# First unit's chain from o to x1 taken batch by batch, weight loads with two semaphores, last expert's add on VectorE, new order tables

## The chip, the cores and the metric

The kernel runs on one core of a Trainium2 chip. The metric is the device time of one execution in microseconds; the median of three runs of the kernel before is 577.14 us. Five engines work side by side, each through its own list in order, and meet at semaphores: TensorE (PE), VectorE (DVE), ScalarE (ACT), GpSimd (POOL) and SyncE (SP), which issues the loads and stores.

## The reference

One decoder layer over x of 16 batches x 128 positions x 256 features. Three parts, each added to its input and normalised:

```python
# attention, 16 heads of 16: causal scores, the 32 largest of each row kept, softmax over them
q, k, v = x @ Wq.T + bq, x @ Wk.T + bk, x @ Wv.T + bv
scores = where(causal, -inf, einsum('bhqd,bhkd->bhqk', q, k) / 4)
attn = softmax(keep_top_32(scores))
x1 = layernorm(x + (attn @ v) @ Wo.T + bo)
# eight experts of 256 -> 512 -> 256, summed with gates of (context, token kind)
h = relu(einsum('edi,bsi->bsed', proj_in, x1)); o = einsum('eid,bsed->bsei', proj_out, h)
gate[e] = sum over k of ctx[b, s, k] where itok[b, k, s] == e
x2 = layernorm(x1 + einsum('bsei,bse->bsi', o, gate))
# Hadamard transform, 4 bit quantised activations, ternary weight
xh = x2 @ H; q = clip(round(xh / scale), -8, 7) * scale
out = layernorm(x2 + q @ ternary(weight).T)
```

## The kernel before

The 16 batches are taken two at a time, in eight **units** v = 0 to 7. A unit has four attention **tiles** k (batch, half of the heads; name 0.3 here for tile 3 of unit 0). A tile goes through scores (PE), copy_scores (ACT), first_max and seven `select` stages of top-8 steps (DVE), exp (ACT), keep (DVE), turn_probs (PE), copy_probs (ACT), attend (PE), normalise (DVE). With all four tiles done the unit has o, and a chain leads to x1: turn_o (PE transposes, recorded at L758), copy_ot (ACT, L653), out_proj (PE, L750), ln1_stats (DVE, L993), rstd1 (POOL, L559), ln1_apply (ACT, L580 and L584), turn_x1 (PE, L758), x1t_high (ACT, L662), x1t_low (DVE, L1019): the last two give x1 transposed as a sum of two float16 parts. Then sixteen expert steps L1 (with relu on ACT and h_low on POOL) alternate with sixteen L2; each is twelve matmuls of 128x256. The gate is applied by gate_out (ACT) and summed by gated_add (POOL), expert by expert. The output part (ln2_stats to store, `OUT_STEPS`) of a unit runs beside the next unit's experts; for the last unit it is done one batch at a time.

K and V of units ahead are computed early into a ring of six (`AHEAD`). The projections, attention outputs, transposes, and the output part share one PSUM bank `ps_misc`: each PE step that takes it waits until the last user has been read (`take_misc`). In the first unit the expert weights are prepared too: load_w (SP) fetches both matrices of an expert into one of two staging buffers, w_squares (ACT, L694) sums their squares, w_sum (PE, L881) adds over partitions, w_scale (DVE, L1041) makes a power of two, w_high (ACT) and w1_low, w2_low (POOL) split the weights in two float16 parts. A buffer is loaded again when both low parts of the expert in it are done.

The order is written out by number: tables `STEADY`, `FIRST` (unit 0), `SECOND`, `LAST`, `FINAL` (last batch) give each step a slot relative to the unit, `PREP` and `AHEAD` those of the weights and of K and V. `build_schedule` places all steps, sorts by slot, and each engine takes its own in that order. No table changes what is computed. The first expert step of a unit waits for `x1t_low`:

```python
if e == 0 and z == 0:
    pe.wait_ge(x1t_low, v + 1)
```

## Time and profile before

| | us |
|---|---|
| three runs, median | 577.14 |
| lowest, highest of them | 575.81, 581.07 |
| profiled execution | 578.48 |
| its span | 576.7 |
| TensorE busy | 524.5 |
| VectorE busy | 444.2 |
| ScalarE busy | 413.6 |
| GpSimd busy | 349.8 |
| mean granted clock of TensorE | 0.964 of full |

The profiled execution has 1.8 us around its span. Busy shares are averages: the program has a ramp in which the first unit's attention and the weights are prepared, a long middle with expert matmuls, and a tail with the output part of the last unit. So the page is read first for the share of each engine and the granted clock by slice, then the windows for the three stages, then the timeline for single steps.

### The profile page before, as it was taken

How to read it: one execution, taken by the hardware profiler on the slowest of the kernel's cores; microseconds unless marked ns; L12 is line 12 of the kernel's file. 1: busy time of each engine (PE TensorE's matmuls, PEld its weight loads, DVE VectorE, ACT ScalarE, POOL GpSimd, SP SyncE). 2: the span in 40 equal slices, each digit the busy share in tenths (PEclk: the TensorE clock that was granted, in tenths of full speed). 3: DMA queues.
4: the chain of work that ended last, by engine and by line, in shares of the span. 5: the costliest groups of instructions: out<-in, count | busy, mean ns of one | idle time of the engine just before them, and what ended most of it. 6: DMA issues, size and time to landing. Idle time of an engine off the chain costs nothing.

```text
span 576.7 us, 22355 instructions
## 1 busy us (share of the span) xinstructions
PE 524.5 (91%) x8180; PEld 449.3 (78%) x8180; DVE 444.2 (77%) x2842; ACT 413.6 (72%) x1004; POOL 349.8 (61%) x358
## 2 busy tenths in 40 slices
PE   4857678999999999999999999999999999999953
PEld 3545557888888888888888888888888888888841
DVE  2798979778889987998899878989899899413114
ACT  3888878766767678768867777778776778567541
POOL 2578556974647565656566654757465746486762
PEclk9878799999999999999999999999999999999985
DMA  7354432000100010000200010002001000000000
GB/s 212 133 167 128 162 116 58 21 3 1 40 19 5 3 35 8 21 3 3 76 20 4 2 59 3 3 3 75 4 3 40 1 21 3 3 1 19 2 18 18
DMA packets 21949, 21.85 MB, mean 38 GB/s; under 512 B 1872, under 2 KB 19792, under 8 KB 21840
## 3 DMA queue, kind: packets, MB, share of 16 engines
q1 hardware_dynamic: 21840, 20.42, 11.4%
q8 instruction: 65, 1.06, 0.8%
q14 instruction: 44, 0.36, 0.2%
HBM read 18.32 MB, written 2.10 MB: 35 GB/s over the span
## 4 chain that ended last, share of the span: by engine, by line
PE 75%; ACT 4%; issue 4%; POOL 3%; DVE 2%; POOLq 0%; ACTq 0%; DVEq 0%
PE ps_o L871 27%; PE ps_z L855 26%; PE ps_misc L750 6%; PE ps_pt L818 5%; PE ps_s L798 4%; PE ps_misc L828 3%; PE ps_misc L733 2%; PE ps_misc L758 2%; POOL h_lo L526 2%; ACT h_raw L674 1%; POOL acc L547 1%; ACT x L580 0%; PE ps_s L807 0%; POOL rstd L565 0%; DVE t L993 0%
## 5 line engine op out<-in xcount | busy, mean ns | idle before, releaser
L526 POOL TENSOR_TENSOR h_lo<-h_raw,h_hi 128x512 f16<-128x512 f32 x128 | 149.2, 1166 | 129.6 <-ACT h_raw L674 128.7
L871 PE MATMUL ps_o<-w_hi,h_lo 128*128 128x256 f16 x512 | 139.7, 273 | 3.4 <-POOL h_lo L526 3.4
L855 PE MATMUL ps_z<-x1t_hi,w_lo 128*128 128x256 f16 x512 | 139.9, 273 | 1.1 <-DVE x1t_lo L1019 1.1
L855 PE MATMUL ps_z<-x1t_lo,w_hi 128*128 128x256 f16 x512 | 139.6, 273 | 0.0
L871 PE MATMUL ps_o<-w_hi,h_hi 128*128 128x256 f16 x512 | 139.6, 273 | 0.0
L871 PE MATMUL ps_o<-w_lo,h_hi 128*128 128x256 f16 x512 | 139.6, 273 | 0.0
L855 PE MATMUL ps_z<-x1t_hi,w_hi 128*128 128x256 f16 x512 | 139.6, 273 | 0.0
L670 ACT ACTIVATE h_hi<-ps_z 128x512 f16<-128x512 f32 x128 | 75.6, 591 | 53.8 <-PE ps_z L855 53.8
L963 DVE MATCH_REPLACE8 taken<-next,taken 128x64 f32<-128x64 f32 (+4 forms) x480 | 110.7, 243 | 0.7 <-issue 0.7
L547 POOL TENSOR_TENSOR acc<-go_sb,acc 128x512 f32<-128x512 f32 x56 | 71.2, 1272 | 32.4 <-ACT go_sb L684 32.4
L958 DVE MAX8 next<-taken 128x8 f32<-128x64 f32 (+4 forms) x480 | 85.4, 245 | 0.0
L674 ACT ACTIVATE h_raw<-ps_z 128x512 f32<-128x512 f32 x128 | 75.6, 590 | 0.0
L637 ACT ACTIVATE pt_sb<-ps_pt 64x512 f32<-64x512 f32 x64 | 37.9, 592 | 34.6 <-PE ps_pt L818 34.2
L684 ACT ACTIVATE go_sb<-ps_o,gate 128x256 f32<-128x256 f32 x128 | 53.4, 470 | 11.3 <-PE ps_o L871 10.0
L871 PEld LDWEIGHTS ps_o<-w_hi,h_lo 128*128 128x128 f16 x512 | 50.0, 98 | 12.3 <-POOL h_lo L526 4.6
L855 PEld LDWEIGHTS ps_z<-x1t_hi,w_lo 128*128 128x128 f16 x512 | 50.1, 98 | 8.2 <-DVE x1t_lo L1019 1.6
L871 PEld LDWEIGHTS ps_o<-w_lo,h_hi 128*128 128x128 f16 x512 | 50.1, 98 | 6.7
L855 PEld LDWEIGHTS ps_z<-x1t_lo,w_hi 128*128 128x128 f16 x512 | 50.1, 98 | 5.9
L871 PEld LDWEIGHTS ps_o<-w_hi,h_hi 128*128 128x128 f16 x512 | 50.1, 98 | 5.8
L855 PEld LDWEIGHTS ps_z<-x1t_hi,w_hi 128*128 128x128 f16 x512 | 50.1, 98 | 5.8
L629 ACT ACTIVATE ps_s<-s_sb,neg_max 128x48 f32<-128x48 f32 (+2 forms) x192 | 51.5, 317 | 0.0
L932 DVE MAX8 top<-s_sb 128x8 f32<-128x16 f32 (+7 forms) x256 | 37.5, 218 | 11.7 <-ACT s_rev L614 11.7
(138 smaller groups left out, 991.2 us busy)
## 6 DMA issues: line engine op xcount, KB each, us to landing
w_raw<-in_w1t SPq DMA_DIRECT2D x8, 512.0 KB, 3.9
w_raw<-in_w2t SPq DMA_DIRECT2D x8, 512.0 KB, 5.0
xt_sb<-in_xt SPq DMA_DIRECT2D x8, 256.0 KB, 3.1
x_sb<-in_x SPq DMA_DIRECT2D x8, 256.0 KB, 3.5
xa_sb<-in_xt SPq DMA_DIRECT2D x7, 256.0 KB, 3.4
out<-out_sb SPq DMA_DIRECT2D x7, 256.0 KB, 2.5
ctx_sb<-in_ctx_w SPq DMA_DIRECT2D x8, 128.0 KB, 3.4
itok_sb<-in_itok SPq DMA_DIRECT2D x8, 128.0 KB, 2.9
```

What stands on the lines that cost most here:

```text
L526: nc.gpsimd.tensor_tensor(h_lo[:, e % 2, 2 * z:2 * z + 2, :], h_raw[:, z, :, :], h_hi[:, e % 2, 2 * z:2 * z + 2, :], ALU.subtract)\
L547: nc.gpsimd.tensor_tensor(acc[:, :, :], go_sb[:, e % 2, :, :], prev[:, :, :], ALU.add)\
L629: last = act.activation(dst, s_sb[:, k % 2, score_at(j):score_at(j) + m], ACT.Exp, bias=neg_max[:, k % 2, j:j + 1], scale=SCALE)
L637: act.activation(pt_sb[0:rows, k % 2, :, HALF * half:HALF * (half + 1), :].rearrange("p h j q -> p j h q"), ps_pt[0:rows, :].rearrange("p ...
L670: act.activation(h_hi[:, e % 2, 2 * z:2 * z + 2, :], ps_z[z][:, :].rearrange("p (c t) -> p c t", c=2), ACT.Relu)\
L674: act.activation(h_raw[:, z, :, :], ps_z[z][:, :].rearrange("p (c t) -> p c t", c=2), ACT.Relu)\
L684: last = act.activation(go_sb[:, e % 2, b, :], ps_o[e % 2][:, b * D:(b + 1) * D], ACT.Copy, scale=gate[:, b, e:e + 1])
L855: last = pe.matmul(ps_z[z][:, d * UT:(d + 1) * UT], w[:, e, c, at:at + P], x[:, c, :], start=n == 0, stop=n == len(terms) - 1)
L871: last = pe.matmul(ps_o[e % 2][:, b * D:(b + 1) * D], h[:, e % 2, c, b * SEQ:(b + 1) * SEQ], w[:, e, c, :], start=n == 0, stop=n == len(te ...
L932: last = V.max(top8[:, k % 2, j, :], s_sb[:, k % 2, score_at(j):score_at(j) + QB * (j + 1)])
L958: last = V.max(next8[:, j, :], t)
L963: last = V.match_replace(t, next8[:, j, :], t, TAKEN)
```

## The change

Five edits. (1) In unit 0 the nine steps of the chain from turn_o to x1t_low (`IN_STEPS`) are done once for batch 0 and once for batch 1, each on its half (`INS`); batch 0's stand in a table of their own, `EARLY`. The other units do them whole, as before; waits that counted units count chains (`chains`). The first expert step waits for both halves. (2) load_w has a semaphore for each of its two loads; the first is issued once w1_low is done, w_squares waits for each when it needs it. (3) In the last unit the eighth expert is scaled and added by VectorE straight from PSUM, one batch at a time (`gated_last`), instead of gate_out on ScalarE and gated_add on GpSimd. (4) For the last unit's two outputs `ffn_residual` moves from GpSimd to VectorE. (5) All tables have new numbers, and each expert's preparation has an offset of its own (`at0` to `at7`).

```diff
+INS = [(0, b, 1) for b in range(UB)] + [(v, 0, UB) for v in range(1, UNITS)]
...
+FINISH = SLOTS + 1
...
+EARLY = STEADY | {
+    "turn_o": 27, "copy_ot": 26, "out_proj": 27.75, "ln1_stats": 27, "rstd1": 33.5, "ln1_apply": 30.5,
+    "turn_x1": 32.5, "x1t_high": 31.75, "x1t_low": 33.5, "ffn": 64, "exp": 4.5, "to_q4": 63.5, "v": 121.25,
...
+    "ffn_abs": -24, "ffn_sum": 40.75, "ffn_ternary": 42.75, "at0": 1.75, "at1": 1, "at2": 0.5, "at3": -0.5,
...
-    ("sp", "load_ctx"), ("sp", "load_x"), ("pool", "x_plus_bo"), ("pe", "turn_o"), ("act", "copy_ot"),
-    ("pe", "out_proj"), ("dve", "ln1_stats"), ("pool", "rstd1"), ("act", "ln1_apply"), ("pe", "turn_x1"),
-    ("act", "x1t_high"), ("dve", "x1t_low"), ("dve", "gate_scale"),
+    ("sp", "load_ctx"), ("sp", "load_x"), ("pool", "x_plus_bo"), ("dve", "gate_scale"),
 )
+IN_STEPS = (
+    ("pe", "turn_o"), ("act", "copy_ot"), ("pe", "out_proj"), ("dve", "ln1_stats"), ("pool", "rstd1"),
+    ("act", "ln1_apply"), ("pe", "turn_x1"), ("act", "x1t_high"), ("dve", "x1t_low"),
+)
+ON_DVE = ("ln3_apply", "ffn_residual")
...
@@ -209,6 +225,10 @@
             elif z == 1:
+                if v == SPLIT and e == EXPERTS - 1:
+                    for b in range(UB):
+                        put(base + at["experts"] + FINISH + b / 8, "dve", "gated_last", v, b)
+                    continue
                 put(s + at["gate_out"], "act", "gate_out", v, e)
@@ -227,10 +247,14 @@
                 put(base + at[name], engine, name, v)
+        for i in (0, 1) if v == 0 else (v + 1,):
+            table = EARLY if i == 0 else at
+            for engine, name in IN_STEPS:
+                put(base + table[name], engine, name, i)
         for o in (v,) if v < SPLIT else (v, v + 1):
...
             for engine, name in OUT_STEPS:
-                put(base + at[name], "dve" if name == "ln3_apply" and v == SPLIT else engine, name, o)
+                put(base + at[name], "dve" if name in ON_DVE and v == SPLIT else engine, name, o)
         if v > 0:
@@ -239,7 +263,7 @@
                 first = max(0, first - PREP_SLOTS * STAGED + max(PREP["w1_low"], PREP["w2_low"]) - PREP["w_squares"])
-            put(first + PREP[name], engine, name, 0, e)
+            put(first + PREP[name] + PREP[f"at{e}"], engine, name, 0, e)
     for engine, name in (("act", "ffn_abs"), ("pe", "ffn_sum"), ("dve", "ffn_ternary")):
@@ -410,10 +436,14 @@
-            if name in OUT_NAMES:
-                _, first, count = OUTS[v]
+            if name in OUT_NAMES or name in IN_NAMES:
+                _, first, count = (OUTS if name in OUT_NAMES else INS)[v]
                 return slice(first, first + count), count
...
+
+        def chains(v):
+
+            return v + 1 if v > 0 else 0
@@ -462,9 +492,9 @@
                     wait(sp, w1_low_ready, e - STAGED + 1)
+                    sp.dma_start(w1_raw[:, e % STAGED, :, :], rows(w1t[e])).then_inc(w1_loaded[e % STAGED], 16)
                     wait(sp, w2_low_ready, e - STAGED + 1)
-                    sp.dma_start(w1_raw[:, e % STAGED, :, :], rows(w1t[e])).then_inc(w_loaded[e % STAGED], 16)
-                    sp.dma_start(w2_raw[:, e % STAGED, :, :], rows(w2t[e])).then_inc(w_loaded[e % STAGED], 16)
+                    sp.dma_start(w2_raw[:, e % STAGED, :, :], rows(w2t[e])).then_inc(w2_loaded[e % STAGED], 16)
                 elif name == "store":
@@ -639,9 +669,10 @@
                 elif name == "ln1_apply":
-                    wait(act, x1t_ready, v)
-                    wait(act, acc_done, EXPERTS * (v - 1) + 1)
-                    layernorm_apply(0, x1, t1, v, x1_ready)
+                    unit = INS[v][0]
+                    wait(act, x1t_ready, chains(unit))
+                    wait(act, acc_done, EXPERTS * (unit - 1) + 1)
+                    layernorm_apply(0, x1, t1, v, x1_ready, batches(name, v)[0])
                 elif name == "ln3_apply":
@@ -649,9 +680,10 @@
                         act.wait_ge(s_vo, 64)
+                    at = columns(batches(name, v)[0])
                     for c in range(CD):
-                        last = act.activation(ot_sb[:, c, :], ps_misc[:, c * UT:(c + 1) * UT], ACT.Identity,
-                                              bias=bv_sb[:, c:c + 1])
+                        last = act.activation(ot_sb[:, c, at], ps_misc[:, c * UT + at.start:c * UT + at.stop],
+                                              ACT.Identity, bias=bv_sb[:, c:c + 1])
                     last.then_inc(ot_copied, 1)
@@ -690,9 +722,10 @@
                     e, = args
-                    act.wait_ge(w_loaded[e % STAGED], 32 * (e // STAGED + 1))
+                    act.wait_ge(w1_loaded[e % STAGED], 16 * (e // STAGED + 1))
                     act.activation(w1_hi[:, e, :, :], w1_raw[:, e % STAGED, :, :], ACT.Square,
                                    accum_out=w_sq[:, e, 0:1])
+                    act.wait_ge(w2_loaded[e % STAGED], 16 * (e // STAGED + 1))
                     act.activation(w2_hi[:, e, :, :], w2_raw[:, e % STAGED, :, :], ACT.Square,
@@ -831,19 +864,20 @@
                 elif name == "turn_o":
-                    pe.wait_ge(o_ready, TILES * (v + 1))
-                    turn(o_sb, ident, ot_ready, ps_misc)
+                    bs, _ = batches(name, v)
+                    pe.wait_ge(o_ready, TILES * INS[v][0] + GROUPS * bs.stop)
+                    turn(o_sb, ident, ot_ready, ps_misc, bs)
                 elif name == "out_proj":
                     pe.wait_ge(ot_copied, v + 1)
-                    rows_by([ot_sb], wo_sb, y_ready)
+                    rows_by([ot_sb], wo_sb, y_ready, batches(name, v)[0])
                 elif name == "turn_x1":
                     pe.wait_ge(x1_ready, v + 1)
-                    turn(x1, ident, x1t_ready, ps_misc)
+                    turn(x1, ident, x1t_ready, ps_misc, batches(name, v)[0])
                 elif name == "L1":
...
                     if e == 0 and z == 0:
-                        pe.wait_ge(x1t_low, v + 1)
+                        pe.wait_ge(x1t_low, chains(v + 1))
                     if v == 0:
@@ -988,12 +1022,14 @@
                     dve.wait_ge(y_ready, v + 1)
-                    dve.wait_ge(xb_ready, v + 1)
-                    wait(dve, x1_ready, v)
-                    V.tensor_tensor(t1[:, :, :], ps_misc[:, :].rearrange("p (b n) -> p b n", b=UB),
-                                    xb_sb[:, :, :], ALU.add).then_inc(t1_ready, 1)
+                    unit = INS[v][0]
+                    dve.wait_ge(xb_ready, unit + 1)
+                    wait(dve, x1_ready, chains(unit))
+                    bs, _ = batches(name, v)
+                    V.tensor_tensor(t1[:, bs, :], ps_misc[:, :].rearrange("p (b n) -> p b n", b=UB)[:, bs, :],
+                                    xb_sb[:, bs, :], ALU.add).then_inc(t1_ready, 1)
                     dve.wait_ge(t1_ready, v + 1)
-                    layernorm_stats(0, t1, v)
+                    layernorm_stats(0, t1, v, bs)
                 elif name == "gate_sums":
@@ -1053,6 +1089,20 @@
                             .then_inc(w_undo_step, 1)
+                elif name == "gated_last":
+                    b, = args
+                    dve.wait_ge(l2_done, RING_STEPS * (v + 1))
+                    dve.wait_ge(acc_done, EXPERTS * v + EXPERTS - 1)
+                    V.scalar_tensor_tensor(acc[:, b, :], ps_o[(EXPERTS - 1) % 2][:, b * D:(b + 1) * D],
+                                           gate[:, b, EXPERTS - 1:EXPERTS], acc[:, b, :], ALU.mult, ALU.add)\
+                        .then_inc(last_added, 1)
+                elif name == "ffn_residual":
+                    bs, _ = batches(name, v)
+                    dve.wait_ge(f_scaled, v + 1)
+                    V.tensor_tensor(t3[:, bs, :], f_sb[:, bs, :], x2[:, bs, :], ALU.add).then_inc(t3_ready, 1)
+                elif name == "ln2_stats" and v >= SPLIT:
+                    dve.wait_ge(last_added, v - SPLIT + 1)
+                    layernorm_stats(1, acc, v, batches(name, v)[0])
                 elif name == "ln2_stats":
```

Where the order moves, at three places. VectorE in the first unit, from the weight scale before the projection's sum to x1t_low; names: `w_ms` is w_scale, `t` with `xb_sb` and `stats` are ln1_stats, `top` is first_max, `p_sb` is keep, `next`, `taken` and `dropped` are select. Before:

```order
L1047 TENSOR_SCALAR w_pow<-w_half 128x2
L993 TENSOR_TENSOR t<-ps_misc,xb_sb 128x512
L908 BN_STATS stats<-t 128x6 x2
L913 BN_AGGR meanvar<-stats 128x2 x2
L932 MAX top<-s_sb 128x8 x8
L972 SCALAR_TENSOR_TENSOR p_sb<-dropped,ps_s 128x48
L974 SCALAR_TENSOR_TENSOR p_sb<-taken,ps_s 128x576
L954 MAX next<-s_rev 128x8
...
L958 MAX next<-taken 128x8 x5
L1019 TENSOR_TENSOR x1t_lo<-ps_misc,x1t_hi 128x512
```

Of the change, the same place (batch 1's half):

```order
L1083 TENSOR_SCALAR w_pow<-w_half 128x2
L1029 TENSOR_TENSOR t<-ps_misc,xb_sb 128x256
L942 BN_STATS stats<-t 128x6
L947 BN_AGGR meanvar<-stats 128x2
L997 MATCH_REPLACE taken<-next,taken 128x64
...
L1006 SCALAR_TENSOR_TENSOR p_sb<-dropped,ps_s 128x48
L1008 SCALAR_TENSOR_TENSOR p_sb<-taken,ps_s 128x576
L966 MAX top<-s_sb 128x8 x8
L988 MAX next<-s_rev 128x8
...
L992 MAX next<-taken 128x8 x5
L1055 TENSOR_TENSOR x1t_lo<-ps_misc,x1t_hi 128x2x128
```

The sum and statistics have half the columns and stand one select stage earlier; between them and x1t_low there is that stage, keep, a first maximum and two select stages. Batch 0's halves stand earlier in the list: the statistics behind the second gate sum, the low part behind the first maximum of the second unit and the weight scale of expert 5.

TensorE in the first unit, from attend of tile 1 to the projection of batch 0 (`wv_sb` is V, `wk_sb` K, `w_sq` a weight sum, `ps_pt` turn_probs). Before:

```order
L828 MATMUL ps_misc<-v_sb,pt_sb 32x17 x32
L733 MATMUL ps_misc<-xa_sb,wk_sb 128x256 x4
L818 MATMUL ps_pt<-ident,p_sb 128x128 x4
L750 MATMUL ps_misc<-wv_sb,xa_sb 128x256 x4
L818 MATMUL ps_pt<-ident,p_sb 128x128 x4
L881 MATMUL ps_o<-w_sq,ones 128x2
```

Of the change:

```order
L861 MATMUL ps_misc<-v_sb,pt_sb 32x17 x32
L766 MATMUL ps_misc<-xa_sb,wk_sb 128x256 x4
L851 MATMUL ps_pt<-ident,p_sb 128x128 x4
L783 MATMUL ps_misc<-wv_sb,xa_sb 128x256 x4
L791 MATMUL ps_misc<-ident,o_sb 128x128 x2
L915 MATMUL ps_o<-w_sq,ones 128x2
L851 MATMUL ps_pt<-ident,p_sb 128x128 x4
L783 MATMUL ps_misc<-wo_sb,ot_sb 128x256 x2
```

The transposes of batch 0's o now stand between V(3) and the weight sum of expert 4, its projection behind the second half of tile 2's probabilities.

VectorE in the tail, from the last two scalings of the ffn output to the end (`rounded` is ffn_scale, `t` from `rounded` is ffn_residual, `stats` ln3_stats, `out_sb` ln3_apply). Before, the residual being GpSimd's:

```order
L1090 SCALAR_TENSOR_TENSOR rounded<-ps_misc,xscale,wscale 128x256
L1090 SCALAR_TENSOR_TENSOR rounded<-ps_z,xscale,wscale 128x256
L908 BN_STATS stats<-t 128x6
L913 BN_AGGR meanvar<-stats 128x2
L908 BN_STATS stats<-t 128x6
L913 BN_AGGR meanvar<-stats 128x2
L920 TENSOR_SCALAR out_sb<-t,meanvar,rstd 128x256 x2
```

Of the change:

```order
L1140 SCALAR_TENSOR_TENSOR rounded<-ps_misc,xscale,wscale 128x256
L1102 TENSOR_TENSOR t<-rounded,x 128x256
L1140 SCALAR_TENSOR_TENSOR rounded<-ps_z,xscale,wscale 128x256
L942 BN_STATS stats<-t 128x6
L947 BN_AGGR meanvar<-stats 128x2
L1102 TENSOR_TENSOR t<-rounded,x 128x256
L942 BN_STATS stats<-t 128x6
L947 BN_AGGR meanvar<-stats 128x2
L954 TENSOR_SCALAR out_sb<-t,meanvar,rstd 128x256 x2
```

The first residual stands between the two scalings, the second behind the first batch's statistics.

## Rows read from the trace of the kernel before

**Rows 1.** The page, part 1: busy us, share of the span, instructions.
```profile
PE 524.5 (91%) x8180; PEld 449.3 (78%) x8180; DVE 444.2 (77%) x2842; ACT 413.6 (72%) x1004; POOL 349.8 (61%) x358
```

**Rows 2.** Windows: us, busy time and instructions of each engine, PEclk, DMA.
```profile
40.00:50.00 10.00, 7.89 (x160) 6.13 (x158) 7.56 (x53) 7.06 (x14) 8.39 (x8) 0.80 0.27 83
70.00:80.00 10.00, 8.63 (x161) 6.69 (x161) 8.07 (x63) 7.20 (x17) 6.48 (x4) 0.77 0.45 145
80.00:90.00 10.00, 6.52 (x105) 4.97 (x105) 7.95 (x40) 8.52 (x19) 5.80 (x7) 1.00 0.46 146
```

**Rows 3.** Windows of TensorE alone, 88.85 to 557.37: the sum.
```profile
sum 468.52, PE 461.82; mean PE 57.73
```

**Rows 4.** TensorE's waits, 88.9 to 557.3: total us, times, longest.
```profile
PE ps_o L871 <- POOL h_lo L526: 3.4, 8, 1.1
PE ps_s L798 <- issue: 2.5, 8, 0.7
```

**Rows 5.** Timeline (start, us, operation, [idle before <-releaser]), waits of VectorE and ScalarE.
```profile
16.85 1.06 ACT L694 ACTIVATE w_hi<-w_raw 128x1024 f16<-128x1024 f32 x1 [0.92 <-DMA w_raw<-in_w2t]
...
19.57 0.16 DVE L1041 TENSOR_SCALAR w_ms<-ps_o 128x2 f32<-128x2 f32 x1 [2.34 <-PE ps_o L881]
...
48.00 0.16 DVE L1041 TENSOR_SCALAR w_ms<-ps_o 128x2 f32<-128x2 f32 x1 [1.60 <-PE ps_o L881]
...
49.34 0.21 DVE L983 RECIPROCAL rsum<-ps_misc 128x8 f32<-128x8 f32 x1 [0.56 <-PE ps_misc L828]
...
76.12 0.21 DVE L983 RECIPROCAL rsum<-ps_misc 128x8 f32<-128x8 f32 x1 [1.86 <-PE ps_misc L828]
...
81.32 0.69 DVE L993 TENSOR_TENSOR t<-ps_misc,xb_sb 128x512 f32<-128x512 f32 x1 [1.11 <-PE ps_misc L750]
```

**Rows 6.** Timeline of TensorE: the second unit's Q.
```profile
26.50 1.99 PE L733 MATMUL ps_misc<-xt_sb,wq_sb 128*128 128x256 f32 x8 [0.23 <-ACT v_sb L606]
```

**Rows 7.** Timeline of VectorE and ScalarE behind the fourth normalise.
```profile
76.64 0.21 DVE L963 MATCH_REPLACE8 taken<-next,taken 128x64 f32<-128x64 f32 x1
...
79.65 0.15 DVE L1041 TENSOR_SCALAR w_ms<-ps_o 128x2 f32<-128x2 f32 x1
...
83.14 1.18 DVE L932 MAX8 top<-s_sb 128x8 f32<-128x16 f32 x8
...
84.83 0.90 ACT L580 ACTIVATE x<-t,minus_mean 128x256 f32<-128x256 f32 x2
...
88.10 0.69 DVE L1019 TENSOR_TENSOR x1t_lo<-ps_misc,x1t_hi 128x512 f16<-128x512 f32 x1 [0.56 <-ACT x1t_hi L662]
```

**Rows 8.** Timeline of TensorE: K(4), V(4) and K(5).
```profile
63.83 3.21 PE L733 MATMUL ps_misc<-xa_sb,wk_sb 128*128 128x256 f32 x8 [4.12 <-DVE o_sb L985]
...
70.63 3.62 PE L750 MATMUL ps_misc<-wv_sb,xa_sb 128*128 128x256 f32 x8
...
82.06 1.99 PE L733 MATMUL ps_misc<-xa_sb,wk_sb 128*128 128x256 f32 x8 [0.78 <-DVE t L993]
```

**Rows 9.** Timeline of ScalarE, GpSimd and VectorE in the tail.
```profile
557.41 0.84 ACT L684 ACTIVATE go_sb<-ps_o,gate 128x256 f32<-128x256 f32 x2 [3.05 <-PE ps_o L871]
...
558.33 1.26 POOL L547 TENSOR_TENSOR acc<-go_sb,acc 128x512 f32<-128x512 f32 x1 [1.29 <-ACT go_sb L684]
...
559.62 0.43 DVE L908 BATCH_NORM_STATS2 stats<-acc 128x6 f32<-128x256 f32 x1 [18.42 <-POOL acc L547]
...
564.18 0.42 DVE L1019 TENSOR_TENSOR x2t_lo<-ps_z,x2t_hi 128x256 f16<-128x256 f32 x1 [0.37 <-ACT x2t_hi L662]
...
568.73 0.48 DVE L1090 SCALAR_TENSOR_TENSOR rounded<-ps_misc,xscale,wscale 128x256 f32<-128x256 f32 x1 [0.54 <-PE ps_misc L750]
...
570.61 0.42 DVE L908 BATCH_NORM_STATS2 stats<-t 128x6 f32<-128x256 f32 x1
...
570.77 0.72 POOL L553 TENSOR_TENSOR t<-rounded,x 128x256 f32<-128x256 f32 x1 [0.75 <-DVE rounded L1090]
```

98 lines of the change are left out of this document (51 added, 47 removed), and 21 rows, old and new, of tables (FINAL, FIRST, LAST, STEADY).

## The prediction, made before the change was run

> **What bounds the kernel now.** I read the page's busy shares first, then the windows, then who waits for whom on TensorE, and only then single instructions of the first 90 us and the last 20. TensorE is busy for 91% of the span, VectorE for 77% [rows 1]. The windows say where: from the first expert matmul at 88.85 us to the last at 557.4 TensorE is busy in 461.8 of 468.5 us [rows 3], and its named waits there are 3.4 us for `h_low` on GpSimd and 2.5 us of "issue" ahead of score matmuls [rows 4]. So the middle is TensorE's own work, and no order of the other engines can take more than these few microseconds out of it. What is left is the ramp and the tail. In the ramp TensorE is the idle one, VectorE the full one: between 40 and 90 us VectorE is busy 7.6, 8.1 and 8.0 of 10 us in the three windows shown, nearly all of the rest being the waits below [rows 2]. It walks a fixed list (the top-32 selection of the first unit's four tiles, parts of the second unit's first tiles, weight scales, gate sums), so the first expert matmul comes when VectorE gets to the end of `x1t_low`. It waits there 2.34 us for the first weight sum, 1.60 for the fourth, 0.56 and 1.86 for the attention output of tiles 1 and 3, 1.11 for the output projection [rows 5]. In the tail (after 557.4) TensorE has nothing left but one batch's short matmuls, and a chain through all engines ends it.
>
> **Loads with a semaphore each, squares and sums earlier.** ScalarE starts the first square 0.92 us late, on the second half of the weights [rows 5]; with its own semaphore the first half's square (1.06 us) fits in that gap: -0.9 us on VectorE's first wait. In ScalarE's and TensorE's lists the fourth expert's squares and sum move ahead of the fourth tile's scores; that takes away the 1.60 us wait and the 0.56 behind it. What is late next is the exponential of tile 2: it needs tile 3's scores copied, and `w_high` of the fourth expert (2 x 1.13 us) now stands ahead of that copy; I give back 0.7. Less 0.4 for the small gaps, VectorE has finished `keep` of tile 2 some 2.0 us earlier. On SP's queue the context's two loads move up from behind expert 4 to behind expert 1's, ahead of the second unit's xt. Q(1), the first reader of that, ran at 26.50 and was waiting for ScalarE, not for the load [rows 6]: nothing.
>
> **The chain from o to x1, batch by batch.** Before, from the end of the last normalise (76.6) to the end of `x1t_low` (88.8) it takes 12.2 us: transposes, copy, projection, sum, statistics, rstd on GpSimd, two rounds of applies (0.90 us the first, of two instructions), transposes, high part, low part 0.69 [rows 7]. With one batch left most of these halve. A half of that size stands in the tail: 0.42 against 0.69 for the low part [rows 7, 9]; at that ratio of 0.6 the chain alone is about 7.5 us. But VectorE has other work listed between the normalise and `x1t_low`: three selection stages (3.0 us, from 76.64 to 79.65 [rows 7]), a weight scale 0.6, the statistics 1.3, then `keep`, a first maximum and two stages (83.14 to 87.54, 4.4 us [rows 7]) and the half low part 0.42: 9.8 us with nothing waited for. So VectorE's list, not the chain, decides: -2.4 us. The price is paid earlier: batch 0's statistics (0.42 + 0.43 + 0.18 and two semaphore waits, 1.3 us) and its low part 0.42 now stand ahead of the last tile: +1.7 us.
>
> **New waits.** `w_sum` of expert 4 now stands behind the transposes of batch 0's o on TensorE, those behind V's copy, and VectorE wants that sum between its two gate sums: nothing if V and K run as at 82.06 (1.99 us), 2.0 us if they run as at 70.63 (3.62) [rows 8]. The sum of expert 5 stands behind batch 0's `turn_x1`, VectorE wants it right after the first maximum: 0 to 1.0. The attention of tile 3 comes behind V(4), which must wait for batch 0's low part: -0.5 to +1.5 on the 1.86 us wait. I take +1.0 for all three, nearer to the low end, since the granted clock is back at 1.00 in the last of the three windows [rows 2] and the slow rate belongs to K(4) and V(4) alone; ends -0.5 and +4.5. V(5) moves from behind the first expert step to ahead of it, 1.73 us of TensorE either way: nothing.
>
> Ramp: -2.0 - 2.4 + 1.7 + 1.0 = **-1.7 us**, ends -5.5 (all waits of VectorE gone) and +2.5.
>
> **The middle.** The tables are new for every unit, but TensorE's matmuls are the same in number and kind. At best its waits go (-4.5), at worst they double (+4.5). I find the same neighbours around most of the steps that it waits for, and take 0.
>
> **The tail.** The last expert's gate (0.84 us on ScalarE) and add (1.26 on GpSimd) put the statistics at 559.62, 2.25 us behind the last matmul [rows 9]. Two `scalar_tensor_tensor` of 128x256 out of PSUM, bounded by the 0.48 us of the same form, take 0.9 together: **-1.3 us**. `ffn_residual` on VectorE: 0.42 in place of 0.72 us, but the second now stands behind the statistics of the first batch, which used to run beside it (570.61, while GpSimd had the residual from 570.77 [rows 9]), so VectorE does residual, statistics, aggregate one after the other and the second batch's aggregate comes 0.2 us later; `rstd3` of the second batch stands behind that of the first on GpSimd, which no longer has the residuals, and takes most of that back. I take 0, ends +0.2 and -0.3. The Trainium skill (GPSIMD Engine Reference, Elementwise — side-by-side cycle accounting) has GpSimd's two-input add at about twice VectorE's time and advises VectorE for elementwise work; the rows agree in kind, 0.72 against 0.42. By that rule alone the move would be worth its 0.3 us and the sum would be 0.3 us lower.
>
> **Sum.** -1.7 + 0 - 1.3 = -3.0 us on the profiled execution's 578.5 us, 575.5. That execution lies 1.3 us above the median of the three runs (577.1), and the saving doesn't depend on it, so the forecast for the median is **574.1 us**.
>
> **Rivals.**
> A, the ramp's waits really vanish: VectorE's list without waits brings the ramp to its low end, and the re-ordered middle gives 1.5 us. For it: VectorE's waits in the ramp add up to 7.5 us [rows 5], and every one belongs to a step that has moved. Against it: three new waits have been put in. -5.5 - 1.5 - 1.3: 568.8 us.
> B, the other side: the half rate of TensorE. TensorE's mean granted clock is 0.80 and 0.77 in two of the windows, so part of each ran at 1.2 GHz; K(4) ran after an idle time of 4.12 us and took 3.21 us, V(4) 3.62, against 1.99 for K(5) in the window at full rate [rows 2, 8]. With batch 0's steps in between, each behind another engine's answer, the shared PSUM bank changes hands three times more often and TensorE gets its long matmuls in smaller pieces. If V(3), K(4) and V(4) all run at half rate, both sums and the attention of tile 3 are late: new waits +4.5 in place of +1.0, and 2 us more for K(5) and the projection's matmuls. It decides once VectorE reaches a weight scale before its sum. 574.1 + 3.5 + 2.0: 579.6 us, slower than before. The Trainium skill (TensorE: Matmul & The Clock Gate, The HAM clock gate) says that the array falls to half rate after idling and regains full rate by sustained work only; the 4.12 us wait and the half rate behind it agree. By that rule a ramp cut into more pieces is the one that runs slower.
> C, the ramp gives nothing: the first expert step comes earlier, but TensorE then waits for the remaining experts' low parts on GpSimd (`w2_low` of expert 6 now stands ahead of `h_low` of expert 1). Only the tail is left: 575.8 us.
> D, the new tables are worse in the middle than the old ones by about half their bound: +2.5: 576.6 us.
>
> **Chances.** Forecast 0.45 (its own range 572 to 576), A 0.22, B 0.11, C 0.12, D 0.10. One per cent, 5.8 us, is about what a measurement of this kernel can tell from no change (its three runs lie 5.3 us apart). Faster by more than that (below 571.4) is nearly all of A and a little of the forecast: 0.25. Slower by more (above 582.9) is B with a worse middle: 0.06. Within: 0.69. The range 567.5 to 579 takes in the forecast, A (with 1.3 us below it, the distance of the lowest of the three runs from their median), C and D, and leaves out most of B.
>
> **What would show it.** Right: the first expert matmul's input (`x1t_low`, second half) ends near 87 us, and the gap from the last normalise to it is near 10 us with VectorE full; VectorE's wait for the fourth weight sum is gone; statistics of the last unit start 1.0 us behind the last matmul. From the first expert matmul to the last, without V(5), it is the same 467 to 469 us. Wrong, if `x1t_low` ends before 85 or after 89 us, if K and V of units 3 to 5 stand in the trace with other durations than at present, or if TensorE's waits between first and last expert matmul differ from 6.7 us by more than 2.

## The result, and the profile after

| | median of | us | ratio of time to the kernel before, 95% interval |
|---|---|---|---|
| kernel before | 21 runs | 577.30 | 1 |
| changed kernel | 21 runs | 579.88 | 1.0038 [1.0022, 1.0053] |

The change makes the kernel slower by 0.38%: 5.8 us above the forecast and 0.9 above its range. The ratio on record is not the quotient of the two medians, which would be 1.0045. "Within 1%" held, the sign and the size did not. The profiled execution took 580.36 us with a span of 578.5 (before 578.48 and 576.7), so the two profiles differ by 1.8 us, in the same direction as the medians.

Part 1 of the page after, against [rows 1]: nothing is heavier than before but TensorE, by 3 us.

```profile
PE 527.6 (91%) x8180; PEld 451.0 (78%) x8180; DVE 441.5 (76%) x2848; ACT 413.5 (71%) x1005; POOL 348.1 (60%) x358
```

The same number of matmuls (8180) takes 3 us more of busy time. The mean granted clock of this profile is 0.960 against 0.964, so more of it ran at the lower clock. The windows of the ramp (columns as in [rows 2]) say where:

```profile
40.00:50.00 10.00, 5.79 (x120) 4.31 (x118) 8.21 (x56) 7.93 (x17) 9.67 (x9) 0.97 0.39 127
50.00:60.00 10.00, 7.69 (x59) 5.74 (x59) 7.49 (x56) 5.45 (x15) 4.30 (x3) 0.66 0.36 113
70.00:80.00 10.00, 8.03 (x156) 6.56 (x156) 7.32 (x51) 5.84 (x11) 6.18 (x5) 0.59 0.32 94
80.00:90.00 10.00, 6.41 (x50) 4.72 (x55) 9.35 (x62) 8.60 (x23) 5.34 (x8) 0.92 0.35 121
```

Between 40 and 50 us TensorE was busy 5.8 us, 2.1 less than before, though the clock was nearly full (0.97); the clock is low in the window behind it (0.66) and again at 70 (0.59, before 0.77). TensorE's own timeline shows what happened there:

```profile
45.16 0.86 PE L831 MATMUL ps_s<-kt_sb,q_spread 32*32 32x16 f32 x58
...
46.12 0.42 PE L861 MATMUL ps_misc<-v_sb,pt_sb 128*32 128x17 f32 x26
50.88 0.73 PE L861 MATMUL ps_misc<-v_sb,pt_sb 128*32 128x17 f32 x38 [4.33 <-issue]
52.26 3.78 PE L766 MATMUL ps_misc<-xa_sb,wk_sb 128*128 128x256 f32 x8 [0.65 <-DVE o_sb L1019]
```

This is the attention of tile 0.1 (tile 1 of the first unit): 64 short matmuls, one wait ahead of the first and none between them. After 26 of them TensorE stands still for 4.33 us, with "issue" as the releaser: nothing that the profile knows held it. The name alone proves little. In the kernel before TensorE stood on "issue" for 2.18 us at 30.68, but at the head of scores 0.2, where the code waits for `keep` of tile 0.0, and that ended at 30.47. Between matmuls that wait for nothing, I took the missing thing to be the next instruction; the runs below test that. In the kernel before the 64 of attention 0.1 ran in one piece. K(3) behind the stop ran at half rate (3.78 us; K at full rate is 1.99 [rows 8]). That was largely so before too:

```profile
50.39 3.37 PE L733 MATMUL ps_misc<-xa_sb,wk_sb 128*128 128x256 f32 x8 [1.10 <-DMA xa_sb<-in_xt]
```

VectorE paid at once. These rows answer to [rows 5], [rows 7] and [rows 9]:

```profile
51.67 0.21 DVE L1017 RECIPROCAL rsum<-ps_misc 128x8 f32<-128x8 f32 x1 [3.26 <-PE ps_misc L861]
...
60.59 0.16 DVE L1077 TENSOR_SCALAR w_ms<-ps_o 128x2 f32<-128x2 f32 x1 [1.27 <-PE ps_o L915]
...
72.58 0.16 DVE L1077 TENSOR_SCALAR w_ms<-ps_o 128x2 f32<-128x2 f32 x1 [0.77 <-PE ps_o L915]
...
79.84 0.21 DVE L1017 RECIPROCAL rsum<-ps_misc 128x8 f32<-128x8 f32 x1 [1.84 <-PE ps_misc L861]
80.08 0.29 DVE L1019 TENSOR_TENSOR o_sb<-ps_misc,rsum 128x128 f32<-128x128 f32 x1
...
89.76 0.41 DVE L1055 TENSOR_TENSOR x1t_lo<-ps_misc,x1t_hi 128x256 f16<-128x256 f32 x1
...
561.47 0.42 DVE L942 BATCH_NORM_STATS2 stats<-acc 128x6 f32<-128x256 f32 x1
```

The wait of the reciprocal, 0.56 before and forecast to vanish, is 3.26. The stretch from the end of the last normalise (80.37) to the end of `x1t_low` (90.17) is 9.8 us, but all of it lies later than forecast. The first expert matmul comes at 93.41 us with V(5) ahead of it; before it was 88.85 with V(5), 1.73 us, behind it. From the end of `x1t_low` TensorE works without a break, on scores and V(5), for 3.24 us; before, 0.05 us of waiting and the 1.73 us of V(5) make 1.8. So of the 2.8 us in the table below, `x1t_low` brings 1.4 and the work behind it the rest, part of it at half rate: the first of it, a turn, took 1.06 us where it was 0.60 before.

| stretch, one profile each | before | after | difference |
|---|---|---|---|
| to the first expert matmul, V(5) counted | 90.6 | 93.4 | +2.8 |
| from there to the last | 466.8 | 467.2 | +0.4 |
| from the last to the end of the span | 19.3 | 17.9 | -1.4 |

TensorE's waits between first and last expert matmul answer to [rows 4]:

```profile
PE ps_o L905 <- POOL h_lo L556: 3.9, 8, 1.1
PE ps_s L831 <- issue: 1.1, 4, 0.3
```

### The profile page after: what moved, and what is told of

Its sections match the earlier page's. It is cut to its first block, busy times and chain, and to the rows that moved or that the text cites. A ratio compares the mean times of both kernels' runs of the same rounds, so it can differ in the third digit from the quotient of the medians.

```text
span 578.5 us, 22360 instructions
## 1 busy us (share of the span) xinstructions
PE 527.6 (91%) x8180; PEld 451.0 (78%) x8180; DVE 441.5 (76%) x2848; ACT 413.5 (71%) x1005; POOL 348.1 (60%) x358
## 3 DMA queue, kind: packets, MB, share of 16 engines
q8 instruction: 65, 1.06, 0.8%
## 4 chain that ended last, share of the span: by engine, by line
PE 71%; POOL 6%; issue 4%; ACT 4%; DVE 3%; POOLq 0%; DVEq 0%; ACTq 0%
PE ps_o L905 25%; PE ps_z L889 24%; PE ps_misc L783 5%; PE ps_pt L851 5%; POOL h_lo L556 4%; PE ps_s L831 4%; PE ps_misc L861 3%; PE ps_misc L766 2%; PE ps_misc L791 2%; POOL acc L577 1%; ACT h_raw L706 1%; POOL rstd L595 1%; ACT ps_s L659 1%; DVE stats L942 1%; PE ps_s L840 0%
## 5 line engine op out<-in xcount | busy, mean ns | idle before, releaser
L992 DVE MAX8 next<-taken 128x8 f32<-128x64 f32 (+4 forms) x480 | 85.4, 245 | 0.0
L889 PEld LDWEIGHTS ps_z<-x1t_hi,w_lo 128*128 128x128 f16 x512 | 50.1, 98 | 7.7 <-DVE x1t_lo L1055 1.2
L905 PEld LDWEIGHTS ps_o<-w_lo,h_hi 128*128 128x128 f16 x512 | 50.1, 98 | 6.9
L905 PEld LDWEIGHTS ps_o<-w_hi,h_hi 128*128 128x128 f16 x512 | 50.1, 98 | 5.8
L889 PEld LDWEIGHTS ps_z<-x1t_hi,w_hi 128*128 128x128 f16 x512 | 50.1, 98 | 5.8
L889 PEld LDWEIGHTS ps_z<-x1t_lo,w_hi 128*128 128x128 f16 x512 | 50.1, 98 | 5.7
```

The lines of the kernel that those rows point to most:

```text
L889: last = pe.matmul(ps_z[z][:, d * UT:(d + 1) * UT], w[:, e, c, at:at + P], x[:, c, :], start=n == 0, stop=n == len(terms) - 1)
L905: last = pe.matmul(ps_o[e % 2][:, b * D:(b + 1) * D], h[:, e % 2, c, b * SEQ:(b + 1) * SEQ], w[:, e, c, :], start=n == 0, stop=n == len(te ...
L992: last = V.max(next8[:, j, :], t)
```

## The experiments

Twelve runs, in three groups, each group on one chip together with the kernel before; the first two rows are those of the result. "Ramp" is the time from the first score matmul to the first expert matmul in the one profile of each kernel; the 1.7 us of V(5) are added where it stands behind that matmul. The ratio rests on 5 to 21 runs, the ramp on one execution.

| kernel | median us | ratio [95%] | ramp us | stop in attention 0.1 |
|---|---|---|---|---|
| before | 577.3 | 1 | 76.6 | none |
| changed | 579.88 | 1.0038 [1.0022, 1.0053] | 79.3 | 4.33 |
| tail_only | 576.39 | 0.9981 [0.9960, 1.0002] | 77.2 | none |
| hold_loads | 578.55 | 1.0021 [0.9996, 1.0047] | 78.6 | 3.24 |
| scores_apart | 577.01 | 0.9983 [0.9962, 1.0005] | 74.1 | none |
| pad_start | 592.40 | 1.0249 [1.0222, 1.0276] | 74.4 | none there |
| burst_before | 577.47 | 0.9991 [0.9965, 1.0018] | 73.6 | none |
| apart_whole | 576.82 | 0.9976 [0.9953, 0.9999] | 74.5 | none |
| loads_before | 578.18 | 0.9989 [0.9965, 1.0014] | 74.8 | none |
| apart_x1_first | 580.37 | 1.0039 [1.0014, 1.0065] | 73.6 | none (0.73 ahead of it) |
| after_again | 579.79 | 1.0030 [1.0006, 1.0055] | 74.4 | 2.41 |
| turns_together | 579.86 | 1.0034 [1.0012, 1.0055] | 76.9 | none |
| order_in_before | 577.94 | 1.0017 [0.9993, 1.0041] | 77.7 | none |
| tail_and_order | 575.92 | 0.9966 [0.9950, 0.9983] | 73.3 | none |

The kernel before had medians of 577.66, 578.47 and 578.28 us beside the three groups, so compare ratios, not medians.

### Is the stop the cause? scores_apart, hold_loads, pad_start, after_again

In the kernel before the short matmuls of scores 0.3 (72 in the trace) stood behind the first turn of tile 0.1's probabilities. The change put them behind the second turn, directly ahead of attention 0.1. **scores_apart** is the changed kernel with that one step put back, on TensorE alone:

```diff
+    moved = ("pe", "scores", 0, (3,))
+    order.remove(moved)
+    order.insert(order.index(("pe", "turn_probs", 0, (1, 0))) + 1, moved)
```

> The changed kernel, with one step moved on TensorE: the scores of tile 3 of the first unit stand behind the first half of tile 1's transposes, as before the change, and not directly ahead of tile 1's attention output. Loads as in the changed kernel. Theory 2 (a burst of short instructions outruns the instruction fetch): the attention output is no longer cut, the first expert matmul comes 2 to 3 us earlier than 93.4. Theory 1 (the packet queues behind the loads): the packet is wanted at about the same count of instructions and the same loads are in flight, so a stall of 2 us or more stays, in the same attention output or just beside it.

Measured: 0.9983. Its timeline of TensorE and of VectorE, the same places:

```profile
41.85 1.21 PE L835 MATMUL ps_s<-kt_sb,q_spread 32*32 32x16 f32 x56
...
46.66 0.74 PE L865 MATMUL ps_misc<-v_sb,pt_sb 128*32 128x17 f32 x64 [0.73 <-ACT v_sb L640]
```

```profile
48.34 0.18 DVE L1021 RECIPROCAL rsum<-ps_misc 128x8 f32<-128x8 f32 x1
...
85.63 0.41 DVE L1059 TENSOR_TENSOR x1t_lo<-ps_misc,x1t_hi 128x256 f16<-128x256 f32 x1
```

All 64 matmuls run in one piece, the reciprocal waits for nothing, and `x1t_low` ends at 86.0, 4.1 us earlier. K(3) behind it took 1.99 us, and from the end of `x1t_low` to the first expert matmul it is 1.9 us in place of 3.2. So one step's place on one engine turns 1.0038 [1.0022, 1.0053] into 0.9983 [0.9962, 1.0005]; the two intervals don't overlap.

**hold_loads** keeps the order and takes the neighbour away: expert 4's two loads, in flight during the stop, are held until attention 0.1 is done.

```diff
                 elif name == "load_w":
                     e, = args
+                    if e == 4:
+                        sp.wait_ge(pv_ready, 2)
```

> The changed kernel, with the two loads of expert 4 on SyncE held until the attention output of tile 1 (first unit) is computed. In the changed kernel TensorE stood still for 4.33 us in the middle of that attention output, after its 26th matmul, with nothing to wait for but its own instructions; one 16 KB packet of the instruction queue moved at 48.0 to 48.5 us, while 1.28 MB of loads issued from 44.02 to 45.90 were in flight. Theory 1 (the instructions' packet is late because it queues behind the loads): the stall shrinks to under 1 us, the first expert matmul comes 2 to 3 us earlier than 93.4, the time falls by 2 to 3 us to about the time of before less 0.5. Theory 2 (the packet is late because scores and attention output of 288 short instructions stand back to back, loads or not): the stall stays over 2 us and the time is that of the changed kernel.

Measured: 1.0021, and the stop is still there, at the same matmul:

```profile
46.34 0.42 PE L863 MATMUL ps_misc<-v_sb,pt_sb 128*32 128x17 f32 x26
50.00 0.70 PE L863 MATMUL ps_misc<-v_sb,pt_sb 128*32 128x17 f32 x38 [3.24 <-issue]
```

From 46.8 to 50.0 the DMA moved 38 packets in all, 37 of data and one of the instruction queue:

```profile
q1 hardware_dynamic: 37, 0.03, 3.3%
q8 instruction: 1, 0.02, 1.9%
```

So the stop does not need data traffic. With it (share 0.83 at 47 to 48 us after) it was 1.1 us longer, but the third profile of this order, below, has the loads again and the shortest stop, so that difference is not shown to be theirs.

**pad_start** leaves every step in its place and puts 128 semaphore increments at the start of TensorE's program.

```diff
+            for _ in range(128):
+                pe.sem_inc(pe_held, 1)
```

> The changed kernel with 128 semaphore increments (nobody waits for them) at the start of TensorE's list, where it waits for its first load anyway: every later instruction stands 128 further on in the stream, half of what a 16 KB packet holds. They may cost 0 to 3 us at the start. Both theories of the instruction fetch: the place of the stall moves, away from the 26th matmul of tile 1's attention output; if it falls where TensorE waits for something else, the time falls by 2 to 3 us less the cost at the start. Rival (the 4.33 us are not instructions but a wait that the profile does not show, such as the bank or a semaphore): the attention output is cut at the same matmul as in the changed kernel.

Measured: 1.0249, because the increments were not free: they run from 0.80 to 20.2 us, one every 0.153 us, and the first matmul starts at 20.48 us in place of 5.64. Less these 14.8 us the median is 577.6, 2.3 below the changed kernel; the other engines had a lead of 14.8 us on TensorE there, so this difference is a hint and no measure. Attention 0.1 runs in one piece, attention 0.2 is cut instead:

```profile
74.17 0.57 PE L861 MATMUL ps_misc<-v_sb,pt_sb 128*32 128x17 f32 x44 [0.28 <-DVE t L1031]
75.95 0.37 PE L861 MATMUL ps_misc<-v_sb,pt_sb 128*32 128x17 f32 x20 [1.21 <-issue]
```

Counting TensorE's records in the trace: the cut in the changed kernel comes after 932 matmul and weight-load instructions and 29 waits and increments, 961; here after 1305, 40 and the 128 added increments, 1473. They lie 512 apart. The page of the changed kernel has 65 packets of 16 KB on the instruction queue (line below) for these 16,360 instructions and 439 waits and increments, one per some 256; with the 128 increments it has 66. The queue's third packet is the one that starts inside the stop in the changed kernel, the fifth here. So both cuts lie on the same grid of two packets' distance: the stop is where one 16 KB piece of the program ends and the next isn't there.

```profile
q8 instruction: 65, 1.06, 0.8%
```

**after_again** is the changed kernel once more.

> The changed kernel, unchanged. Theory, the stop of TensorE belongs to this order of its instructions: a second profile shows it at the same matmul, after the 26th of the 64 of attend 0.1, for 3 to 5 us on 'issue', with one 16 KB packet of the instruction queue inside the stop; time 579.0 to 580.5, ratio 1.002 to 1.006. Rival, chance of one execution: no stop there this time, x1's low half ends near 86.5 to 87.5 in this profile, and the slower median is not due to it.

Measured: 1.0030, the cut after the same 26 matmuls:

```profile
46.33 0.42 PE L861 MATMUL ps_misc<-v_sb,pt_sb 128*32 128x17 f32 x26
49.16 0.52 PE L861 MATMUL ps_misc<-v_sb,pt_sb 128*32 128x17 f32 x38 [2.41 <-issue]
```

The place recurs in 3 of 3 profiles of this order, the length varies: 4.33, 3.24, 2.41. In each one the piece's packet started 2.3 to 2.5 us before the matmuls went on (48.4, 47.7 and 46.8 us; in pad_start 73.8, 2.2 before). But this profile also speaks against making the stop the whole of it: its ramp was 74.4 us, as short as that of scores_apart, since the reciprocal waited 1.76 only and the last tile's 1.14 in place of 1.84. This execution was then slow in another way (585.7 us; granted clock 0.95 from 90 us on, and a matmul of 128x256 took 278 ns in place of 273), which its kernel's median does not share.

### Are two short runs back to back enough? burst_before, order_in_before, turns_together

**burst_before** puts scores 0.3 directly ahead of attention 0.1 in the kernel before; its copy on ScalarE moves along.

```diff
+    for moved, behind in (
+            (('pe', 'scores', 0, (3,)), ('pe', 'w_sum', 0, (3,))),
+            (('act', 'copy_scores', 0, (3,)), ('act', 'w_high', 0, (3,))),
```

> The kernel before, with the scores of tile 0.3 moved on TensorE from behind the first turn of tile 0.1's probabilities to directly ahead of attend of tile 0.1 (and their copy on ScalarE behind the fourth expert's w_high, as the change has it), so that its two long runs of short matmuls (68 and 64) stand back to back. Theory, instruction fetch: the 64 matmuls of attend stall in the middle, 1 to 4 us on 'issue', about 2 us later than they stand now (near 50); the reciprocal behind them on VectorE waits 1.5 to 4 us longer than its 0.56, the first expert matmul starts 1.5 to 4 us later than 88.85, and the time is 578.5 to 581, ratio 1.003 to 1.007. Rival, the loads: in this kernel expert 4's loads are not issued until about 3 us later, so the burst alone does nothing: no wait on 'issue' above 0.7, time within 1 us of 577.3.

Measured: no stop, 0.9991. The theory as I had put it, the two runs alone, falls. `x1t_low` ended at 85.8 us here, 3 us before the 88.8 of the kernel before, and the median is 1.0 us lower only, within the noise: the ramp of one profile does not carry over to the median us for us.

**order_in_before** gives the kernel before the whole of the change's order between attention 0.0 and K(3): first turn, V(2), sum, second turn, scores 0.3, attention 0.1.

```diff
+            (('pe', 'turn_probs', 0, (1, 1)), ('pe', 'w_sum', 0, (3,))),
+            (('pe', 'scores', 0, (3,)), ('pe', 'turn_probs', 0, (1, 1))),
+            (('act', 'copy_scores', 0, (3,)), ('act', 'w_high', 0, (3,))),
+            (('act', 'copy_probs', 0, (1, 1)), ('act', 'copy_v', 2, ())),
```

> The kernel before with TensorE's steps between attend 0.0 and K(3), and ScalarE's copies that go with them, in the order of the change: first turn of tile 0.1, V(2), sum 3, second turn, scores 0.3, attend 0.1. Theory, the order alone makes the stop: attend 0.1 stops on 'issue' for 2 to 5 us, the reciprocal behind it on VectorE waits as much, the first expert matmul comes 2 to 4 us later than 88.85; time 578.5 to 581, ratio 1.001 to 1.006. Rival, it takes the change's other moves (the scores of tiles 0.1 and 0.2 behind the sum and the turns) too: no stop above 0.7 us, time within 1 us of the kernel before.

Measured: no stop, 1.0017, not told apart from 1.

**turns_together** is the changed kernel with the second turn moved up behind the first; the two short runs stay together.

```diff
+            (('pe', 'turn_probs', 0, (1, 1)), ('pe', 'turn_probs', 0, (1, 0))),
```

> The changed kernel with the second turn of tile 0.1's probabilities moved on TensorE from ahead of scores 0.3 to behind the first turn; scores 0.3 and attend 0.1 still stand back to back, as in burst_before, which did not stop. Theory A, two short runs back to back are enough: the stop of 3 to 5 us stays, time 579 to 580.5. Theory B, what matters is how many instructions are left to issue after the last step that waits (two turns, V(2) and a sum stand ahead in this order, and the sequencer gets past the point at which the next 16 KB are asked for earlier): the packet is moved before 45, there is no stop above 1 us, x1's low half ends 3 to 4 us earlier than 90.2, and the time is 576.5 to 577.5, ratio 0.997 to 1.000.

Measured: no stop, as theory B said, but 1.0034, as theory A said; the packet came at 48.0 us and not before 45 as B wanted, and `x1t_low` ended at 90.4. V(2) and the fourth sum now stand behind a turn that waits for ScalarE's copy (2.71 us on TensorE), and VectorE waits for the sum instead:

```profile
46.43 0.63 PE L857 MATMUL ps_pt<-ident,p_sb 128*128 128x128 f32 x4 [2.71 <-ACT pt_sb L673]
```

```profile
50.17 0.16 DVE L1083 TENSOR_SCALAR w_ms<-ps_o 128x2 f32<-128x2 f32 x1 [3.27 <-PE ps_o L921]
```

3.27 us here, 3.26 there: VectorE loses the same, whatever it waits for. What sets the stop apart is when the packet of that piece was moved, against the start of scores 0.3. It came before or with them where there was no stop: in scores_apart (41.9 us, scores at 41.85), burst_before (40.2, 46.3), order_in_before (47.2, 49.6), turns_together (48.0, 50.1) and tail_and_order (43.5, 47.0), and 1.4 to 3.2 us behind them in the three that stopped (46.8 to 48.4, scores at 45.2 to 45.4). Scores and the 26 matmuls then use up the rest of the piece in 1.4 us. The place of the cut is the same in all orders but pad_start's, the kernel before included: 909 records stand ahead of attention 0.1 in each, so the piece ends behind the same matmul, and only the packet's time against TensorE's differs. In the kernel before it came at 42.3 us, 6 us ahead of attention 0.1; in turns_together it was as late as in those that stopped, but TensorE came to scores 0.3 some 5 us later. What makes the chip ask for a piece early or late stays open.

### What are the parts worth? tail_only, loads_before, apart_whole

**tail_only**: the kernel before with the last expert's last addition and the last residual on VectorE.

```diff
+                    for b in range(UB):
+                        put(base + at["experts"] + FINISH + b / 8, "dve", "gated_last", v, b)
...
-                put(base + at[name], "dve" if name == "ln3_apply" and v == SPLIT else engine, name, o)
+                put(base + at[name], "dve" if name in ON_DVE and v == SPLIT else engine, name, o)
```

> The kernel before with the tail's two edits alone (last expert added on VectorE, the last two residuals on VectorE, residual of the second batch ahead of the first batch's statistics), all tables and the rest as before. The tail's term of the sum was -1.3 us, and the changed kernel's tail measured 17.9 us from the last matmul's end to the end of the span against 19.3. Theory: this gain is real and independent of the ramp, so 1.2 to 1.5 us faster than before, with the same ramp (first expert matmul near 88.9 us). Rival: the tail's gain is an accident of what ran beside it there, and the time is the same as before.

Measured: 0.9981 [0.9960, 1.0002], 1.1 us, with 1 just inside the interval; from the last matmul to the end of the span 18.1 us in place of 19.3. The first expert matmul came at 91.25, but the first score matmul of this profile was 1.8 us later too.

**loads_before**: the kernel before with the semaphores for each half alone.

```diff
-                    act.wait_ge(w_loaded[e % STAGED], 32 * (e // STAGED + 1))
+                    act.wait_ge(w1_loaded[e % STAGED], 16 * (e // STAGED + 1))
...
+                    act.wait_ge(w2_loaded[e % STAGED], 16 * (e // STAGED + 1))
```

> The kernel before, with the loads' part of the change alone: a semaphore for each half of an expert, the first half's load issued ahead of the wait for the second buffer, the squares of the first half not waiting for the second. Theory, the loads bring what was forecast (2.0 us at the first expert matmul, since the waits of w_ms on TensorE's sums, 2.34 and 1.60, shrink by about 1 each): time 575.3 to 576.5. Rival, VectorE's later waits take it back (the order was made for the old loads): the first expert matmul within 0.5 us of 88.85, the time within 0.7 us of 577.3.

Measured: 0.9989. The rival holds: the first expert matmul comes at 88.98 us, and the median is 0.3 us from that of the kernel before in the same group, 578.47. The first sum was no earlier (`w_ms` waited 3.13 us), the fourth's wait was 1.14 in place of 1.60. The first wait says little about the semaphores: it was 1.30 us in tail_and_order, which has the old loads, and 3.08 in tail_only, which has them too.

**apart_whole**: scores_apart with the first unit's chain in one piece again.

```diff
-INS = [(0, b, 1) for b in range(UB)] + [(v, 0, UB) for v in range(1, UNITS)]
+INS = [(v, 0, UB) for v in range(UNITS)]
...
-            return v + 1 if v > 0 else 0
+            return v
```

> The changed kernel with the scores of tile 0.3 moved away from attend 0.1 (as in scores_apart), and with the first unit's chain from the turn of o to x1's low half whole again, at the places that batch 1's half has. Theory, the split is worth what was forecast for it (chain of 12.2 us behind the last normalise against 9.8): the whole x1t_lo ends 1.5 to 3 us later than the 86.0 of scores_apart, and the time is 578 to 580 against its 577.0. Rival, the split is worth nothing, since VectorE's list sets that end and batch 0's half puts 1.7 us into it: x1t_lo ends at 85 to 86.5 and the time is within 1 us of 577.0.

Measured: 0.9976 against 0.9983, the ramp 74.5 against 74.1 us. From the end of the last normalise to that of `x1t_low` it is 12.0 us, against 9.8 in scores_apart, as forecast; `x1t_low` ended at 87.3, with the first score matmul 2.2 us later than there. The split by batch, the title of the change, is worth nothing that can be measured: counted from the first score matmul `x1t_low` ends 0.9 us earlier without it, so batch 1's shorter end is paid for by batch 0's half ahead of the last tile.

### Versions that were to be better: apart_x1_first, tail_and_order

**apart_x1_first**: scores_apart with x1's second half ahead of other work.

```diff
+            (('act', 'w_high', 0, (6,)), ('act', 'x1t_high', 1, ())),
+            (('dve', 'x1t_low', 1, ()), ('dve', 'select', 1, (1, 0))),
```

> The changed kernel with the scores of tile 0.3 apart from attend 0.1, and x1's second half ahead of two pieces of other work: on ScalarE the seventh expert's w_high (2.2 us) behind ln1_apply(1), copy_k(5) and x1t_high(1), on VectorE x1t_low(1) one step of the selection earlier. In scores_apart rstd of batch 1 was ready at 81.4 and ln1_apply started at 82.39, x1t_lo ended at 86.04. If the chain sets the end, x1t_lo ends 1.0 to 1.5 us earlier and the first expert matmul comes 1.0 to 1.5 us before 87.93; the time is 575.5 to 576.2, ratio to before 0.996 to 0.998. Rival: POOL's w_lo of expert 6, now later by some 1 us, or the scores and V(5) ahead of the first expert matmul on TensorE take it back, and the time is that of scores_apart, 577.0.

Measured: `x1t_low` ends 0.5 us earlier, the first expert matmul comes 0.5 us earlier (87.46), and the kernel is slower, 1.0039. From the first expert matmul to the last it takes 471.9 us, 468.6 in scores_apart. Behind it the delayed work comes due, inside the stretch that is TensorE's own:

```profile
94.16 0.27 PE L913 MATMUL ps_o<-w_hi,h_lo 128*128 128x256 f16 x1 [1.20 <-DVE w_half L1088]
...
102.03 1.12 PE L859 MATMUL ps_pt<-ident,p_sb 128*128 128x128 f32 x4 [2.47 <-DVE p_sb L1016]
```

In scores_apart that last wait was 1.1 us; and the turn behind it took 1.12 us where 0.6 is full rate: the clock had fallen to half again (0.83 over 100 to 110 us, 1.00 in scores_apart).

**tail_and_order**: tail_only with burst_before's two moves.

> A version made of what the runs showed to be worth something: the kernel before with the last expert's last addition and the residual on VectorE (tail_only, ratio 0.9981) and with scores 0.3 moved as in burst_before (ratio 0.9991, whose profile had x1's low half at 85.8 against 88.8). If the two add up, the ratio to before is 0.996 to 0.998, the time 575.0 to 576.3. Rival: both were noise of 0.25% and it is the kernel before, ratio 0.999 to 1.001.

Measured: 0.9966 [0.9950, 0.9983], 575.92 us, where the changed kernel in the same group had 579.79. It beats both. `x1t_low` ends at 85.4, the last unit's statistics follow the last addition at once:

```profile
554.23 0.88 DVE L1073 SCALAR_TENSOR_TENSOR acc<-ps_o,gate,acc 128x256 f32<-128x256 f32 x2 [16.21 <-PE ps_o L884]
555.02 0.41 DVE L921 BATCH_NORM_STATS2 stats<-acc 128x6 f32<-128x256 f32 x1
```

## Why the prediction was wrong, by its own steps

**Loads and squares earlier, -2.0: the order's part right but for one clause, the semaphore's not shown.** The first wait fell from 2.34 to 1.30 us, near the 0.9 forecast, but by the runs above that need not be the semaphore's doing. The fourth weight sum was there 2.7 us earlier (45.26 for 48.00) with no wait. But the step says "that takes away the 1.60 us wait and the 0.56 behind it", and the 0.56 became 3.26. This is the step that failed: a wait that was to go cost 2.7 us more than before, and took back all that the two earlier sums had brought (1.04 and 1.60). The prediction's own sign of being wrong, `x1t_low` after 89 us, is there (90.2). The step looked at whom VectorE waits for and at when that work could start, and took a run of matmuls on TensorE for something that runs through once started. The page before had the same 65 instruction packets, and [rows 4] had 2.5 us of "issue" ahead of scores, which I named and did not ask about. The trace before has no stop inside a run, though, so length and place could not have been read from it.

**The chain by batch, -2.4 + 1.7: right in the parts.** Normalise to the end of `x1t_low` took 9.8 us for 9.8 forecast, with VectorE busy 9.35 of the 10 us from 80 to 90; apart_whole shows 12.0 for the whole chain, and that the net, forecast at -0.7, is at most that.

**New waits, +1.0 with ends -0.5 and +4.5: too small, and the largest was not among them.** The two weight scales waited 1.27 and 0.77 (forecast up to 2.0 and 1.0), the last tile 1.84 for 1.86. With the 3.26 that is 5.3 us of VectorE's time in place of 1.0. By subtraction, without the 3.26 `x1t_low` would have ended at 86.9, against 87.1 forecast; in scores_apart it ended at 86.0. The low value was taken because "the slow rate belongs to K(4) and V(4) alone", and that was misread: K(3) took 3.37 us in the kernel before and K(2) 3.78, and from 50 to 60 us, a window that was not looked at, the granted clock was 0.83. V(5), "nothing", is part of the 1.4 us more that TensorE needs between `x1t_low` and the first expert matmul.

**Middle 0: right**, 467.2 against 466.8 us. **Tail -1.3: right**, 17.9 against 19.3; the statistics start 0.84 us behind the last matmul (forecast 1.0), and tail_only by itself has a tail 1.2 us shorter and 1.1 us in the median, the latter at the edge of its noise.

**Rival B said 579.6 and got the number, with a chance of 0.11, but not the cause.** Its mark, VectorE at a weight scale before its sum, is there. Its matmuls are not: K(4) took 2.68 us (before 3.21 [rows 8]), V(4) 3.78 (3.62), V(3) 2.32 (1.89). K(3) behind the stop took 3.78, but 3.37 before; it is 1.99 in scores_apart. And where the order is all the change's but for scores 0.3, the ratio is 0.9983: the smaller pieces that B blames are in that kernel too, and so are two of the new waits, 0.77 us and the last tile's 1.76; the 1.27 us for the sum of expert 4 is gone with the stop (its timeline has no wait there). B's argument may hold in general form: the median granted clock over a kernel's runs goes with its time in the clearest cases, 0.970 in tail_and_order, 0.965 before, 0.961 in after_again and turns_together, though scores_apart has 0.9635 and is not slower. If it has two levels only, 1.2 and 2.4 GHz, and a span near 577 us these are, as an estimate, 35, 40 and 45 us of half rate. From 50 to 60 us, behind the stop, the granted clock was 0.66; in scores_apart, without the stop, it was 1.00. The Trainium skill (TensorE: Matmul & The Clock Gate, The HAM clock gate) has the array at half rate after idling; that stretch agrees. C (575.8, only the tail) and D (576.6, the middle worse) did not happen; A needed every wait of the ramp gone, and none of the runs came near its 568.8.

**The range.** Its upper end left B out by design. The bound of the new waits (+4.5) lay in the range of the sum, the bound of a wait inside a run was in none. The ramp's ends, -5.5 and +2.5, are not sums of its terms either: with the ends of the new waits these give -3.2 and +1.8.

What is not settled: what sets the time at which a piece of the program is asked for, and how the median's loss divides between the stop and the half rate. The change of one step gives 0.9983 for 1.0038, that is shown. That the whole difference comes through the stop is argued from single profiles, where ramps vary by several us from one execution to the next, and two things speak against it: after_again has the stop and a ramp of 74.4 us, turns_together and apart_x1_first have no stop and are as slow as the change.

## What to carry to other kernels

Before putting two runs of short matmuls together on TensorE, count instructions and not microseconds: 72 and 64 matmuls are 272 instructions, more than a 16 KB piece holds, used up in some 2 us. Together they stopped TensorE in one order here and in four others not, so it is a thing to look for in the profile after and no rule. After a reordering, look first for "issue" in the middle of a group that has no waits; it is a wait that no list of dependences shows. An edit at the end of the program (the last addition on the engine that needs it) kept its shorter tail in every profile here (17.2 to 18.1 us against 19.3), while what the edits in the ramp brought at their own place was taken back by waits elsewhere.

## What the runs showed of the hardware that was not expected

- TensorE's instructions come in 16 KB packets, some 256 instructions each, and it can run out of them: stops of 4.33, 3.24 and 2.41 us at the same instruction of the same order, 1.21 us two pieces further in pad_start. In other orders the piece's packet came earlier or TensorE later, and there was no stop. The matmuls go on 2.2 to 2.5 us after the packet starts, though the packet itself takes about 1 us.
- A semaphore increment in TensorE's own stream costs 0.153 us: 128 of them ran from 0.80 to 20.2 us and put the first matmul 14.8 us later, in time in which I had thought it idle.
- One profile of the changed kernel had a granted clock of 0.95 from 90 us to its last matmul, where the others have 1.00, with TensorE busy 99% of the time. It took 585.7 us where the median is 579.8.
